# Products of each level in two halves, with other work between them, in the delta loop of a two-layer network

## The reference

```
for each token t:
    s = s * alpha[..., None]
    pred = jnp.einsum('bhk,bhkv->bhv', kt, s)
    s = s + (beta * kt)[..., None] * (vt - pred)[:, :, None, :]
    out = jnp.einsum('bhk,bhkv->bhv', qt, s)
y = y * rsqrt(mean(y * y) + EPS) * head_norm_w
y = x + y @ Wo * gate
z = _rms(y, ff_norm_w)
y = y + silu(z @ Wff1) * (z @ Wff3) @ Wff2
```

## Time and profile before

| what | us |
|---|---|
| median of three runs | 3167.55 |
| lowest and highest of them | 3156.91 and 3168.99 |
| the profiled execution | 3158.89 |
| its span | 3157.1 |
| delta loop, from first diagonal product of pass 0 to that of pass 7 | 1286.93 to 2446.91 |

### The profile page before, as it was taken

The page is one execution under the profiler, slowest core; times in us unless marked ns, Lnnn a source line. Parts: engine busy times, 40 slices in busy tenths (PEclk is TensorE's granted clock), DMA queues, the critical chain, the costliest instruction groups (busy, mean ns, idle before and its releaser), DMA issues. The chain is left out here.

```text
span 3157.1 us, 73508 instructions
## 1 busy us (share of the span) xinstructions
PE 2443.4 (77%) x31207; PEld 1699.1 (54%) x31207; DVE 1571.4 (50%) x3747; ACT 994.8 (32%) x1934; POOL 679.8 (22%) x816
## 2 busy tenths in 40 slices
PE   7988999897674704798979888888889787947665
PEld 4666666666553301465555555555556556646553
DVE  4465554554624394636364545445353722575334
ACT  3344343432122701233333333343333341311111
POOL 1011010100154201222221222213031300103553
PEclk9899897996697856798989898989998985555555
DMA  3000000000211103000000000000000002000113
GB/s 138 8 8 8 1 8 5 2 1 1 75 37 46 54 0 133 15 6 19 2 22 2 22 3 19 6 19 6 15 6 2 6 2 83 2 27 25 38 36 102
DMA packets 43654, 79.45 MB, mean 25 GB/s; under 512 B 6116, under 2 KB 27372, under 8 KB 40516
## 3 DMA queue, kind: packets, MB, share of 16 engines
q1 hardware_dynamic: 36292, 60.30, 5.5%
q0 software_dynamic: 7040, 14.43, 1.7%
HBM read 48.56 MB, written 26.15 MB: 24 GB/s over the span
## 5 line engine op out<-in xcount | busy, mean ns | idle before, releaser
L2640 DVE COPY_PREDICATED delta_neg_a_and_p_t<-delta_level_int,bank 128x256 f32<-128x256 uint8 x384 | 178.4, 534 | 267.4 <-PE bank L2204 266.4
L2561 POOL TENSOR_TENSOR delta_scaled_beta_k<-delta_scaled_beta_k,delta_decays 128x256 f32<-128x256 f32 x160 | 121.5, 759 | 567.7 <-DVE weights_sb L2662 362.5
L2228 PEld LDWEIGHTS bank<-delta_inverse,delta_neg_a_and_p_t 64*64 64x64 f32 x5120 | 183.3, 150 | 43.3 <-issue 42.9
L2228 PE MATMUL bank<-delta_inverse,delta_neg_a_and_p_t 64*64 64x64 f32 x5120 | 206.4, 237 | 0.0
L2204 PE MATMUL bank<-weights_sb,delta_scaled_beta_k 64*64 64x64 f32 x6144 | 131.9, 231 | 78.1 <-DVE delta_neg_a_and_p_t L2640 76.8
L2204 PEld LDWEIGHTS bank<-weights_sb,delta_scaled_beta_k 64*64 64x64 f32 x6144 | 111.2, 141 | 109.3 <-DVE delta_neg_a_and_p_t L2640 89.1
L2415 ACT ACTIVATE delta_two_less_ax<-bank 128x512 f32<-128x512 f32 x160 | 94.8, 597 | 238.2 <-PE bank L2228 238.1
L303 PE MATMUL bank<-attn_z_self_t,weights_sb 128*128 128x256 f32 x512 | 148.8, 441 | 16.6 <-DVE attn_cross_values L741 13.0
L683 POOL TENSOR_TENSOR attn_probs<-attn_probs,attn_row_sum 128x512 f32<-128x512 f32 x64 | 65.3, 1042 | 392.5 <-DVE attn_row_sum L766 392.5
L312 PE MATMUL bank<-attn_w_value_out,attn_z_self_t 128*64 128x512 f32 x512 | 143.8, 688 | 2.1 <-DVE attn_z_value_out L706 1.4
L2250 PEld LDWEIGHTS bank<-delta_two_less_ax,delta_inverse_t 64*64 64x64 f32 x4096 | 126.8, 139 | 22.7 <-issue 17.8
(11 more groups left out here) (508 smaller groups left out, 5386.0 us busy)
## 6 DMA issues: line engine op xcount, KB each, us to landing
delta_spikes<-front_drive SPq DMA_DIRECT2D x8, 1024.0 KB, 8.7
weights_sb<-delta_spikes SPq DMA_DIRECT2D x8, 1024.0 KB, 5.1
weights_sb<-in_w_moe_dram SPq DMA_DIRECT2D x1, 4352.0 KB, 14.8
z_rows<-moe_z_all SPq DMA_DIRECT2D x16, 256.0 KB, 2.3
weights_sb<-moe_outs SPq DMA_DIRECT2D x8, 512.0 KB, 7.2
weights_sb<-in_w_delta_dram SPq DMA_DIRECT2D x1, 2816.0 KB, 10.5
weights_sb<-in_ctx_tok_dram SPq DMA_DIRECT2D x8, 264.0 KB, 6.0
attn_x_channels<-in_x_dram SPq DMA_DIRECT2D x8, 256.0 KB, 3.0
```

What stands on the lines that cost most here:

```text
L2228: last = pe.matmul(out_[rows(sg), u], AP[rows(sg), hp, eo, b4, 0, :], X[rows(sg), hp, u], start=False, stop=True, skip_group_check=True)
L2561: pool.tensor_tensor(r_[:, :, 0, :], r_[:, :, 0, :], a_[:, :, 1, 0:1].to_broadcast([128, T // (2 * c), c]), ALU.mult)
L2640: last = dve.copy_predicated(second(AP[:, hp, eo, :, :, :].rearrange("p b i n -> p (b i) n"), c), m_, PAIR[hp % 2][eo][:, :].rearrange("p ...
```

## The change

It changes the order in which instructions stand on three engines. None is added or taken away.

- TensorE: `diag`, `products`, `xw`, `t_ss` and `f_kq` take the list of `hp` or `j` they do. The diagonal and levels 0 and 1 are issued in two halves with two fills behind each; levels 2 to 5 in two halves with two X W products of the level before behind each. The fills that stood between products and X W (`f_al`, `t_ff`) move behind both, `values` moves ahead of the second `f_ct`.
- ScalarE: the X copies `x_out` of levels 3 and 4 move ahead of one `t_silu` and of `t_silu`, `f_au` and a table load.
- VectorE: the gating product becomes a function of its own, `t_gated`, ahead of the masked copies of level 1; the `t_hidden` steps move earlier or between other steps.

```
                         if core:
-                            diag(it)
+                            diag(it, 0, 1)
                         if tail:
-                            t_ss(it - 1)
-                        if core:
-                            products(it, 0)
+                            t_ss(it - 1, 0, 1)
+                        if core:
+                            diag(it, 2, 3)
+                        if tail:
+                            t_ss(it - 1, 2, 3)
+                        if core:
+                            products(it, 0, 0, 1)
                         if front:
-                            f_kq("k", it + 1)
+                            f_kq("k", it + 1, 0, 1)
+                        if core:
+                            products(it, 0, 2, 3)
+                        if front:
+                            f_kq("k", it + 1, 2, 3)
                         if tail:
                             t_wo(it - 1)
...
                             ax(it, 1)
-                            products(it, 2)
+                            products(it, 2, 0, 1)
+                            xw(it, 1, 0, 1)
+                            products(it, 2, 2, 3)
+                            xw(it, 1, 2, 3)
                         if front:
                             f_al(it + 1, 2)
-                        if core:
-                            xw(it, 1)
-                        if front:
                             f_al(it + 1, 3)
...
                         if core:
-                            products(it, 4)
+                            products(it, 4, 0, 1)
+                            xw(it, 3, 0, 1)
+                            products(it, 4, 2, 3)
+                            xw(it, 3, 2, 3)
                         if tail:
                             t_ff(it - 1, 1)
-                        if core:
-                            xw(it, 3)
                         if front:
                             f_bc("bk", it + 1)
...
                             t_dn(it - 1)
+                        if core:
+                            values(it)
                         if front:
                             f_ct(it + 1, 1)
                         if core:
-                            values(it)
                             y(it)
@@ ScalarE
                         if tail:
                             t_silu(it - 1, 2)
+                        if core:
+                            x_out(it, 4)
+                        if tail:
                             t_silu(it - 1, 3)
                         if ahead:
                             f_au(it + 2)
                         act.preload_act_table(ACT.Sigmoid)
                         if core:
-                            x_out(it, 4)
                             w_out(it, 5)
@@ VectorE
                                 first_inverse(it, hp)
+                        if tail:
+                            t_gated(it - 1)
+                        if core:
                             for hp in range(HDP):
                                 masked(it, 2, hp)
                                 scale(it, 1, hp)
...
+                        if tail:
+                            t_hidden(it - 1, 0)
+                        if core:
                             for hp in range(HDP):
                                 masked(it, 5, hp)
                                 scale(it, 4, hp)
-                        if tail:
-                            t_hidden(it - 1, 0)
-                            t_hidden(it - 1, 1)
-                        if core:
                             for hp in range(HDP):
                                 turned(it, 3, hp)
+                        if tail:
+                            t_hidden(it - 1, 1)
                         if front:
                             f_bc("bk", it + 1)
```

More of the change, by code:

```diff
@@ L2101, in f_au, with f_kq @@
                         pe.matmul(out_[0:64, :], col("wau", 0, 64), h[:, g % 3, :], start=True, stop=True).then_inc(s["au_ps"], 1)
-                    def f_kq(kind, g):
-                        for j in range(HDP):
+                    def f_kq(kind, g, *js):
+                        for j in js:
                             out_ = fill(kind, g, j)
@@ L2134, in f_ct, with t_ss @@
                         pe.matmul(out_[:, :], wD[:, 6, j * 128:(j + 1) * 128], spk[:, j, :], start=False, stop=True).then_inc(s["bt_ps"], 1)
-                    def t_ss(g):
-                        for j in range(HDP):
+                    def t_ss(g, *js):
+                        for j in js:
                             out_ = fill("ss", g, j)
@@ L2182, in pair_free, with diag @@
                         return PAIR[hp % 2]
-                    def diag(g):
-                        for hp in range(HDP):
+                    def diag(g, *hps):
+                        for hp in hps:
                             two = pair_free(g, 0, hp)
@@ L2193, in diag, with products @@
                             last.then_inc(s["products"], 1)
-                    def products(g, l):
+                    def products(g, l, *hps):
                         c = 1 << l
-                        for hp in range(HDP):
+                        for hp in hps:
                             two = pair_free(g, l + 1, hp)
@@ L2230, in ax, with xw @@
                             last.then_inc(s["w_ps"], 1)
-                    def xw(g, l):
-                        for hp in range(HDP):
+                    def xw(g, l, *hps):
+                        for hp in hps:
                             n = 20 * g + HDP * (l - 1) + hp
@@ L2300, in _ @@
                         if core:
-                            products(it, 1)
+                            products(it, 1, 0, 1)
                         if front:
-                            f_kq("q", it + 1)
+                            f_kq("q", it + 1, 0, 1)
+                        if core:
+                            products(it, 1, 2, 3)
+                        if front:
+                            f_kq("q", it + 1, 2, 3)
                             f_al(it + 1, 0)
@@ L2339, in _ @@
                         if core:
-                            products(it, 5)
+                            products(it, 5, 0, 1)
+                            xw(it, 4, 0, 1)
+                            products(it, 5, 2, 3)
+                            xw(it, 4, 2, 3)
                         if tail:
@@ L2691, in t_y @@
                             .then_inc(s["wo_rd"], 1)
+                    def t_y(g):
+                        yf = y2[:, :, :].rearrange("p i d -> p (i d)")
                         dve.wait_ge(s["wo_rd"], g + 1)
@@ L2816, in _ @@
                                 masked(it, 6, hp)
-                        if tail:
-                            t_hidden(it - 1, 2)
-                            t_hidden(it - 1, 3)
-                        if core:
                             for hp in range(HDP):
                                 turned(it, 4, hp)
+                        if tail:
+                            t_hidden(it - 1, 3)
                         if front:
```

17 lines of the change are left out of this document (11 added, 6 removed).

## The result

The changed kernel takes 3076.32 us (median of three runs, 3069.27 to 3087.04) where the kernel before takes 3167.55: a ratio of 0.9725, with a 95% interval from 0.9669 to 0.9781. The forecast was 3087, with a range from 3045 to 3125. The profiled execution's span went from 3157.1 to 3074.5 us.

A forecast was written before the change was run, and what follows sets the result against it. TensorE was taken to set the pace, with 23.9 us idle in a pass; terms summed to 11.9 us a full pass, 71 for six, 80 with passes 0 and 7, off 3167.55: forecast 3087 us, range 3045 to 3125.

The forecast's parts named there:

- levels 0 and 1, diagonal to A X: First stretch of a pass: VectorE's chain and the gate release TensorE earlier; 6.7 us, bounds 0.75 and 7.5.
- level 2: Masked-copy wait of 1.0 us goes, but TensorE then waits for the transposes of z; 0.4 us taken.
- level 3: Halves with X W products between remove the wait for masked copies, nothing else moves; 1.0 us.
- level 4: Masked-copy wait 1.0 and second feed-forward fill's wait 2.44 go, about 0.4 back at the second bk fill; 3.0 us.
- level 5: Masked-copy wait 0.4, next fill bank 0.4 and X copy behind the table load 0.67 go; 1.5 us.
- values, to the next diagonal: Value copies stand behind the beta activation on ScalarE, so y waits 2.9 us against 2.17; costs 0.7 us.
- 0.8 us for a lower clock: First stretch: at the lower clock one fill in four costs 0.9 more, so 6.7 taken where 7.5 was worked out.
- the rival of the clock that comes back: Half of 31 us at 1.2 GHz in a pass goes; 6.4 us more a pass, 3036 us; chance 0.10.
- the 0.03 that I had named as a sign of being wrong: Mean granted clock of a pass stays near 0.91; a move by more than 0.03 means the prediction is wrong.
- the slower rival: Levels 2 to 5: unbroken 6.2 us runs of small products lose the clock; 48 us slower, 3216 us; chance 0.03.
- Pass 0: First pass, without tail, so no gate or feed-forward waits and nothing between its diagonal halves; gain about 3 us.
- pass 7: Last pass, without front, keeps the gains of levels 2 to 5; about 6 us.

The follow-up runs named there:

- e_early: Kernel before with only diagonal, levels 0 and 1 in halves with fills between, and the gating product ahead of the level-1 copies; 3116.24 us, ratio 0.9835.
- e_table: Changed kernel with ScalarE's load of the silu table behind the four W copies of level 3 instead of ahead of them; 3071.49 us, ratio 0.9713.
- e_act_values: Changed kernel with ScalarE's four value copies ahead of the beta activation of the second ct/bt fill; 3062.91 us, ratio 0.9688.
- e_best: Changed kernel with value copies before the beta activation, table load behind level 3's W copies, third decay fill between level 2's second half and X W; 3042.22 us.
- e_gate: Kernel before with one move, the gating product ahead of the level-1 masked copies on VectorE, nothing in halves; 3152.08 us, ratio 0.9966.
- e_hidden_only: Kernel before with only VectorE's new order of the t_hidden steps and the level-4 and level-5 masked copies around them; 3166.52 us, ratio 1.0014.
- e_hidden_back: Changed kernel with all four t_hidden steps on VectorE back where they stood before the change; 3112.42 us, ratio 0.9836.
- e_values_back: Changed kernel with the value products back behind the second ct/bt fill; 3070.08 us, ratio 0.9693.

## Why the prediction was right, step by step

The time was forecast 10.7 us too high, well within its range. Some of this is the median it started from: 3167.55 us in three runs, where 9 to 13 later runs of that kernel had medians of 3160 to 3163. By its terms, per full pass:

| term | forecast | measured |
|---|---|---|
| levels 0 and 1, diagonal to A X | 6.7 (0.75 to 7.5) | 8.1 |
| level 2 | 0.4 | 0.3 |
| level 3 | 1.0 | 0.9 |
| level 4 | 3.0 | 3.1 |
| level 5 | 1.5 | 1.9 |
| values, to the next diagonal | -0.7 | -1.0 |
| full pass | 11.9 | 13.4 |

- **Levels 0 and 1: the mechanism was right, the size just above its bound.** The steps were: VectorE's masked copy of the second pair ends 0.75 us earlier; one last product, two q and two decay fills follow it; 0.8 us for a lower clock. That copy ended at 1801.76, 32.5 us after the start of pass 3 at 1769.27, and in the changed kernel TensorE's product behind it starts at 1777.84, 31.3 us after its first diagonal product at 1746.52, so 1.2 us earlier; and the four fills run at full clock (two times 1.98 us). The 0.8 us taken off for the clock was not needed in any of the six passes. It can be: eight of the kernels run here have this order in the stretch, and in 4 of their 48 full passes (one each in e_early, e_table, e_act_values and e_best) the last q fills ran at the lower clock and the stretch took 37.4 to 38.3 us. The e_gate run bears out the rest.
- **The idle time was misjudged, and hid its error.** I forecast that idle would fall from 23.9 to some 13 us and the clock would stay near 0.91; idle is 16.3, and the clock 0.93 in pass 3 and 0.94 over six. The head-norm sums between the diagonal halves now wait 2.4 us for ScalarE, which I didn't price, and three waits for masked copies are left. They cost next to nothing: in that stretch TensorE waits for VectorE, and fills that run faster ahead of the last wait only turn busy time into idle time. In all 48 passes of the eight kernels with the early halves the second q fill, which waits for the gating product, starts 28.3 to 28.4 us after the first diagonal product, whether TensorE waited 0.6 us for it or 3.4. What then decides the end is seen in two passes of e_act_values, the fifth and the first, from the first diagonal product to the A X products:

```profile
2049.00:2084.77 35.77, 27.97 (x445) 16.27 (x445) 33.48 (x52) 13.88 (x22) 15.08 (x18) 0.90 0.09 31
1434.80:1472.81 38.01, 27.86 (x445) 15.75 (x445) 35.62 (x61) 13.88 (x22) 17.21 (x21) 0.91 0.10 32
```

 Both have nearly the same clock and the same busy time. In the first row the lower clock falls on two k fills and the output projection, ahead of the last wait, and the stretch is as short as at 0.95. In the second it falls on the last products and two q fills, and costs 2.2 us. So of the 4.8 us less busy only what lies behind the last wait is a gain: three q fills took 4.41 us before and take some 3.0 at the full clock's 0.99 each, so about 1.4 of the 8.1 us are the clock's (my sum had them in it, as it took the new fills at 0.99). Beyond that the rival of the clock that comes back did not come true: the clock did rise, from 0.91 to 0.94 over the six passes, just under the 0.03 that I had named as a sign of being wrong, but only in the first stretch. Elsewhere it is lower or within 0.01 of before (AX3 to 4 had 0.94 and has 0.91; AX4 to 5 0.91 and 0.88), so its 6.4 us on top of the rest did not come.
- **Level 4: the right number from a wrong step.** I gave 2.44 us to the feed-forward wait, "since its bank is now emptied ahead of VectorE's masked copies", as a gain of the t_hidden move alone. In e_hidden_only that wait is gone too, and the pass is no faster. In e_hidden_back the wait is down to 0.36 without the move. What the move does is to bring the transposes, and with them the multiplication by bk or bq, in time for fills that the halves let TensorE reach earlier. That the term came out within 0.1 us is chance. Level 5, at 1.9, holds the same joint gain, of which my 1.5 named only part.
- **Level 2 and level 3** came as worked out. The transposes of z do wait for VectorE (0.9 us), and keeping the third decay fill between the products and X W removes that.
- **Values: the step was right.** y waits 2.7 us for ScalarE, where 2.9 was forecast. Against e_values_back, which differs in this move alone, the way from A X of level 5 to y is 0.8 us longer, where 0.7 was forecast; against the kernel before it is 0.2 longer. The rest of the measured 1.0 is y at the lower clock in more passes, which e_values_back has as well, and which I had not priced.
- **Long runs of small products did not lose the clock.** This was the slower rival. Below is first 1827.00 to 1834.66 of the changed kernel, products, X W products and two fills in one run, then the later bk fills and the A X products behind them; then level 5, up to the bq fills, these fills, and the A X products behind them:

```profile
1827.00:1834.66 7.66, 7.66 (x261) 6.36 (x261) 7.43 (x15) 2.99 (x5) 4.30 (x8) 1.00 0.01 3
1836.61:1840.00 3.39, 3.39 (x6) 0.95 (x7) 1.92 (x3) 0.00 (x0) 0.00 (x0) 0.86 0.03 5
1840.00:1845.43 5.43, 5.43 (x69) 3.88 (x68) 0.69 (x1) 1.02 (x2) 0.00 (x0) 0.50 0.00 0
1846.71:1858.68 11.97, 11.97 (x302) 8.32 (x300) 6.59 (x14) 4.78 (x8) 0.00 (x0) 1.00 0.01 3
1858.68:1862.49 3.81, 3.81 (x9) 1.19 (x9) 2.06 (x3) 1.97 (x2) 0.00 (x0) 1.00 0.01 2
1863.00:1866.70 3.70, 3.70 (x65) 3.15 (x62) 0.28 (x1) 0.60 (x1) 0.00 (x0) 0.55 0.02 4
```

 The long runs have the full clock throughout. It is in the bk fills, 16 rows deep, that the clock falls (0.86), and the A X products behind them run at 0.50. TensorE stood idle for 0.83 us just ahead of that window, but the bq fills, as deep, are the clearer case: TensorE is busy without a pause from 1836.61 to behind 1866.70, and the clock falls at the end of these fills all the same. That their depth is the reason is not shown: no run changes it.

Pass 0 gained 1.3 where I took 3 and pass 7 6.6 where I took 6. The first tells little: e_gate's pass 0, the same as before the change, took 146.98 us against 143.92. The order itself puts one more limit on what could be tried: with levels 4 and 5 in halves, X W must have W and the transposes while ScalarE still serves t_silu, whose fill stands behind them; I argue from this that the x_out moves belong to the halves, but did not run it without them.

## What to carry to other kernels

Splitting a step over few buffers into halves, with other work between them, pays what that work covers, and it can need a new order on the engines that serve it: here halves without VectorE's move, and the move without halves, gained nothing in levels 4 and 5, and together 5 us a pass. In levels 2 and 3 halves alone were enough, for 1.3 us. After such a change look in each in-order queue for what stands ahead of the copy that is waited for (a table load, an activation of another fill); two such swaps, each on its own, were worth 2.9 and 1.7 us a pass, and with a third edit 5.2. And don't read a fall of busy time as a gain, or a rest of idle time as a loss, in a stretch in which another engine's chain sets the end.

## What the runs showed that I had not expected

- The clock at y depends on what comes before it by more than the length of the wait. With a wait of 2.2 to 2.7 us y ran at the lower clock in 1 of 6 passes in the kernel before, 4 in the changed one, 5 in e_values_back and 3 in e_table; with no wait (e_act_values, e_best) in none of 12. In e_hidden_only, where y's surroundings are those of the kernel before, it was 4 of 6. What decides between the passes stays open.
- In the first stretch the halves raised the granted clock from 0.80 to 0.95 while the gating product alone left it at 0.80. The Trainium skill (TensorE: Matmul & The Clock Gate, Part 1: The HAM clock gate) says that the engine's activity releases the clock. This stretch agrees with it weakly, as TensorE was busy for 72% of it before and for 75% after. The rows at 1858.68 and 1863.00 do not, if busy time is taken for activity: the engine was busy throughout, and the clock fell.
- Small products of two kinds can alternate on TensorE without a seam: groups of 32 products and of 31 or 32 X W products (two records each) took 1.1 and 2.0 us in turn, with no idle time between.
